# A gated cross-attention and expert block on one core: one start-up sum moved from VectorE to accumulating DMAs, three pieces of TensorE's order moved, and the last output add split

## The reference, cut to what matters

```python
x = x + tanh(g_xattn[0]) * attention(layernorm(x), ctx, wq, wk, wv, wo, q_norm_w, k_norm_w)
x = x + tanh(g_ffn[0])   * experts(layernorm(x), A, B, Wr)

# attention: x (16, 128, 1024), ctx (16, 128, 1024), 32 query heads, 8 key heads of 128
q, k = rmsnorm(x @ wq.T), rmsnorm(ctx @ wk.T)      # per head
out  = softmax(q @ k.T / sqrt(128)) @ (ctx @ wv.T)
return out @ wo.T
# experts: 64 experts of rank 16, the 16 best of a token are used
gates = softmax(top_k(x @ Wr.T, 16));  h = x @ A.T        # (tokens, 64 * 16)
return 2 * (h * gates) @ B
```

## Time and profile before

| | us |
|---|---|
| median of 3 runs (2317.69 to 2320.09) | 2319.02 |
| the profiled execution | 2318.4 |
| its span, first to last instruction | 2316.6 |
| PE busy | 2261.6 |
| DVE busy | 1597.6 |
| ACT busy | 1183.9 |
| POOL busy | 1144.8 |
| mean granted clock of PE, share of 2.4 GHz | 0.997 |

### The profile page before, as it was taken

The page is one execution under the profiler, slowest core; times in us unless marked ns, Lnnn a source line. Parts: engine busy times, 40 slices in busy tenths (PEclk is TensorE's granted clock), DMA queues, the critical chain, the costliest instruction groups (busy, mean ns, idle before and its releaser), DMA issues.

```text
span 2316.6 us, 35630 instructions
## 1 busy us (share of the span) xinstructions
PE 2261.6 (98%) x11615; PEld 1906.0 (82%) x11615; DVE 1597.6 (69%) x2669; ACT 1183.9 (51%) x3773; POOL 1144.8 (49%) x1735
## 2 busy tenths in 40 slices
PE   6999999999999999999999999999999999999999
PEld 5887887888888878888888788888888887888787
DVE  7558558777777797777777954755756878555755
ACT  5546546666666676666666732422424335333421
POOL 3666566666555555555555453233232664534221
PEclk9999999999999999999999999999999999999999
DMA  5688466767667367764322635645557566323643
GB/s 198 218 245 296 150 197 232 212 165 204 183 170 191 121 212 205 230 179 128 110 91 92 209 100 164 182 127 166 162 152 216 186 217 255 128 92 136 237 164 136
DMA packets 177062, 408.78 MB, mean 176 GB/s; under 512 B 11824, under 2 KB 77616, under 8 KB 159664
## 3 DMA queue, kind: packets, MB, share of 16 engines
q1 hardware_dynamic: 169392, 351.97, 44.1%
q0 software_dynamic: 7488, 54.53, 12.9%
HBM read 282.72 MB, written 190.84 MB: 204 GB/s over the span
## 4 chain that ended last, share of the span: by engine, by line
PE 84%; DVE 4%; POOL 4%; issue 3%; ACT 3%; DMA 2%; SPq 0%; POOLq 0%; ACTq 0%; DVEq 0%
PE bank L769 23%; PE bank L771 23%; PE bank L770 23%; PE bank L827 4%; PE bank L835 2%; PE bank L815 2%; DVE t_lo L1320 1%; PE bank L852 1%; PE bank L851 1%; PE bank L850 1%; ACT t_hi L1024 1%; POOL s_hi L1811 1%; DVE s_lo L1320 1%; DMA t_raw<-combos 1%; DMA staged<-in_w_q 1%
## 5 line engine op out<-in xcount | busy, mean ns | idle before, releaser
L769 PE MATMUL bank<-t_hi,s_hi 128*128 128x512 f32 x2688 | 1084.0, 403 | 30.7 <-DVE t_lo L1320 17.3
L771 PE MATMUL bank<-t_hi,s_lo 128*128 128x512 f32 x2688 | 1053.8, 392 | 0.0
L770 PE MATMUL bank<-t_lo,s_hi 128*128 128x512 f32 x2688 | 1050.9, 391 | 0.0
L769 PEld LDWEIGHTS bank<-t_hi,s_hi 128*128 128x128 f32 x2688 | 507.2, 189 | 128.1 <-issue 32.3
L771 PEld LDWEIGHTS bank<-t_hi,s_lo 128*128 128x128 f32 x2688 | 505.8, 188 | 110.7
L1320 DVE TENSOR_TENSOR s_lo<-staged,s_hi 128x512 fp32r<-128x512 f32 x672 | 525.0, 826 | 88.9 <-ACT s_hi L1035 86.9
L770 PEld LDWEIGHTS bank<-t_lo,s_hi 128*128 128x128 f32 x2688 | 507.5, 189 | 90.3
L1035 ACT CAST s_hi<-staged 128x512 fp32r<-128x512 f32 x434 | 250.2, 623 | 184.9 <-POOL staged L1801 71.5
L1782 POOL TENSOR_SCALAR small<-small 128x4 f32<-128x4 f32 (+1 forms) x192 | 75.9, 395 | 446.9 <-ACT small L1131 341.4
L1799 POOL TENSOR_TENSOR staged<-staged 128x512 f32<-128x512 f32 x86 | 115.3, 1340 | 365.5 <-DMA staged<-heads 196.9
L1463 DVE SCALAR_TENSOR_TENSOR probs<-bank,small,mask 128x128 f32<-128x128 f32 x512 | 143.9, 343 | 87.1 <-POOL small L1789 43.6
(11 more groups left out here) (143 smaller groups left out, 2894.7 us busy)
## 6 DMA issues: line engine op xcount, KB each, us to landing
heads<-heads SPq DMA_DIRECT2D x128, 256.0 KB, 4.3
staged<-in_w_q SPq DMA_DIRECT2D x32, 768.0 KB, 5.2
staged<-heads SPq DMA_DIRECT2D x32, 768.0 KB, 6.9
sums<-sums POOLq DMA_DIRECT2D x24, 1024.0 KB, 8.0
t_raw<-in_sets SPq DMA_DIRECT2D x20, 1024.0 KB, 7.1
t_raw<-combos SPq DMA_DIRECT2D x19, 1024.0 KB, 8.6
xt<-x_columns SPq DMA_DIRECT2D x8, 1792.0 KB, 6.8
combos<-in_sets POOLq DMA_DIRECT2D x14, 1024.0 KB, 10.2
```

The source lines that it names most:

```text
L769: nc.tensor.matmul(out, s_hi[w][:, cols], high, start=start, stop=False, skip_group_check=True)
L770: nc.tensor.matmul(out, s_hi[w][:, cols], low, start=False, stop=False, skip_group_check=True)
L771: done = nc.tensor.matmul(out, s_lo[w][:, cols], high, start=False, stop=at == 3, skip_group_check=True)
```

## The change

Five edits:

1. Tile 6 of the first set: `b21` is loaded straight into `t_raw[6]`, and POOL issues three accumulating transfers of 1 MB from DRAM into it (pieces 2, 3 and 0), each after the one before it has landed (`t4_added`). DVE's sum (line 1625) goes. ACT's `first_t(6)` waits for all three.
2. Transposes of the keys and of the first half of the x rows stand after product 3 instead of 2 in entries 8 and 9.
3. In entry 80 the router stands after product 4, the transpose of the scores after product 5, and DVE's `choose(0, 0)` in the slot of product 6.
4. The scratch tensor `xt` is laid out by partition, so that a tile of sets 2 and 3 is read in pieces of 8 KB instead of four of 2 KB.
5. In the last entry the `usum` part of the last result is scaled and added early, and the bank part straight from PSUM.

```diff
-        self.xt = scratch("xt", 2, 7, 4, P, HALF)
+        self.xt = scratch("xt", 2, 7, P, 4, HALF)
...
+    def router_beat(e):
+        return 4 if e == A0 else 3
...
-                src = d.xt[tau - 2, k].rearrange("a p c -> p a c")
+                src = d.xt[tau - 2, k]
...
             if tau == 1:
-                sp.wait_ge(t0_combo, 4)
                 src = weights(1, 0)
...
-        sp.dma_start(b21_again[:, :, :], b_in[1]).then_inc(again_in[1], 16)
+        sp.dma_start(t_raw[6][:, :, :], b_in[1]).then_inc(again_in[1], 16)
...
-                if e and j == 2:
+                if e and j == (3 if e in (8, 9) else 2):
                     key_columns(e - 1, 0)
                     x_columns(e - 1, 0)
...
-                if j == 3:
+                if j == router_beat(e):
                     router(e - A0)
-                if j == 4:
+                if j == router_beat(e) + 1:
                     score_rows(e - A0)
...
-                act.wait_ge(t0_combo, {2: 1, 3: 2, 1: 3, 6: 4}[k])
+                if k == 6:
+                    act.wait_ge(t4_added, 48)
+                else:
+                    act.wait_ge(t0_combo, {2: 1, 3: 2, 1: 3}[k])
...
+                if j == router_beat(e) + 1:
+                    router_scores(e - A0)
                 if j == 4:
-                    router_scores(e - A0)
                     rank_tile(e - A0)
...
+                if i == PAIRS - 1:
+                    nc.vector.scalar_tensor_tensor(yr[b][1][:, left], usum[:, :], tg2[:, :], yr[b][1][:, left], ALU.mult, ALU.add).then_inc(y_part, 1)
+            if j == 7 and i == PAIRS - 1:
+                dve.wait_ge(prod, plan.prod[e, 6])
+                dve.wait_ge(y_part, 1)
+                nc.vector.scalar_tensor_tensor(yr[b][1][:, left], bank[3][:, :], tg2[:, :], yr[b][1][:, left], ALU.mult, ALU.add).then_inc(y_set, 1)
...
-        dve.wait_ge(again_in[1], 16)
-        dve.wait_ge(t0_combo, 3)
-        nc.vector.tensor_tensor(t_raw[6][:, :, :], b21_again[:, :, :], t_raw[1][:, :, :], ALU.add).then_inc(t0_combo, 1)
         first_t(1)
...
+                if j == router_beat(e) + 2:
                     choose(i, 0)
...
+        def first_set_sum():
+            for n, b in enumerate((2, 3, 0)):
+                if n:
+                    pool.wait_ge(t4_added, 16 * n)
+                else:
+                    pool.wait_ge(again_in[1], 16)
+                nc.gpsimd.dma_start(t_raw[6][:, :, :], d.sets[0, b].rearrange("p (k c) -> p k c", k=4), accum_op=ALU.add,
+                                    max_dma_last_dim=8192).then_inc(t4_added, 16)
+
         sums(0)
+        first_set_sum()
```

More of the change, by code:

```diff
@@ L274, in program @@
     xo = m.put("x_columns", [P, 7, 4, S])
-    b11_again, b21_again = m.over("b11_again", [P, 4, HALF], xo_at), m.over("b21_again", [P, 4, HALF], pc_at)
+    b11_again = m.over("b11_again", [P, 4, HALF], xo_at)
     first_ahead = m.over("first_ahead", [P, 4, HALF], pc_at)
@@ L325, in program @@
     again_in, b12_in = [sem(f"again_in{w}") for w in range(2)], sem("b12_in")
+    y_part = sem("y_part")
     t_hi_done, t_lo_done, t0_combo = sem("t_hi_done"), sem("t_lo_done"), sem("t0_combo")
+    t4_added = sem("t4_added")
     st_in, st12_in = sem("staged_in"), sem("staged12_in")
@@ L481, in load_first_ahead @@
                 sp.wait_ge(xt_out, 64)
-                src = d.xt[0, 0].rearrange("a p c -> p a c")
+                src = d.xt[0, 0]
             sp.dma_start(first_ahead[:, :, :], src).then_inc(first_ahead_in, 16)
@@ L555, in columns_out @@
             sp.wait_ge(xo_pool, 2 * u + 2)
-            sp.dma_start(d.xt[u // 4, :, u % 4].rearrange("k p c -> p k c"), xo[:, :, :, :].rearrange("p k b q -> p k (b q)")).then_inc(xt_out, 16)
+            sp.dma_start(d.xt[u // 4, :, :, u % 4].rearrange("k p c -> p k c"), xo[:, :, :, :].rearrange("p k b q -> p k (b q)")).then_inc(xt_out, 16)
         def heads_out(w):
@@ L1597, in y_rows @@
                 nc.vector.scalar_tensor_tensor(yr[b][0][:, right], ct[1][:, :], tg2[:, :], yr[b][0][:, right], ALU.mult, ALU.add).then_inc(y_set, 1)
-            if j == 7:
+                if i == PAIRS - 1:
[4 more added lines that the diff above has]
+                nc.vector.scalar_tensor_tensor(yr[b][1][:, left], bank[3][:, :], tg2[:, :], yr[b][1][:, left], ALU.mult, ALU.add).then_inc(y_set, 1)
+            elif j == 7:
                 result21(e, ct[2][:, :])
@@ L1603, in first_t @@
         def first_t(k):
-            if k in (1, 3):
-                dve.wait_ge(t0_combo, 4 if k == 1 else 3)
+            if k == 3:
+                dve.wait_ge(t0_combo, 3)
             dve.wait_ge(t_hi_done, plan.t_fill(0, k))
```

## The result

| | before | after |
|---|---|---|
| median of 6 runs each, us | 2317.97 (2317.28 to 2320.09) | 2327.18 (2325.74 to 2327.85) |
| the profiled execution, us | 2318.4 | 2327.46 |
| its span, us | 2316.6 | 2325.7 |
| mean granted clock of PE | 0.997 | 0.995 |

The ratio is 1.0038, with an interval of 1.0028 to 1.0048: slower by 9.2 us. The forecast's sum was 2325.1, slower.

A forecast was written before the change was run, and what follows sets the result against it. PE bounds the kernel, busy 2261.6 of 2316.6 us. The terms 8.4 + 1.9 - 1.7 - 1.8 - 0.7 = +6.1 gave 2324.5 from the profiled execution, 2325.1 with the runs' median; range 2317.5 to 2331, the forecast's own 2321.5 to 2329.

The forecast's parts named there:

- Edit 1, what goes: At the start, removing DVE's addition of 2.28 us gains 0, since PE is held by its own spare matmuls.
- The first issue at 21.7: At the start, POOL issues the first accumulating transfer when piece b21 has landed, at 21.7 us.
- The first transfer, 9.0: At the start, the first accumulating transfer takes 9.0 us, since the last start-up loads are still arriving.
- The other two, 8.0 each: At the start, the second and third accumulating transfers take 8.0 us each, so tile 6 is whole at 46.7.
- Cast, `t_lo`, bank: 5.1: From landing at 46.7, adding 1.9, 2.3 and 0.9 puts product 6 at 51.8 against 43.39: +8.4 us.
- The clock, +1.9: PE idles 9.5 us before product 6 and drops to 1.2 GHz, costing 1.9 us; bounds 0 and 2.
- Edit 3, -1.8: In entry 80, `choose` moved behind the `s_lo` PE waits for gives -1.8 us; filling the router gap alone gives nothing.
- Edit 5, -0.7: At the end, the addition goes and the scaling starts at 2312.01, giving -0.7 us.
- A (nearly hidden): Rival at the start: transfers cost only 5.75 us each, product 6 at 44.1, kernel at 2315.5; chance 0.12.
- B (the moved pieces give nothing): Rival in entries 9 and 80: the wait only turns up a product later, kernel at 2328.6; chance 0.12.
- C (the issues are held up): Rival at the start: POOL's issues are stretched by 1 to 2 us each, +3 to +4, 2329; chance 0.11.
- D: Rival at the start: the third wait is met early, or a piece runs together; chance 0.02.

The follow-up runs named there:

- The two-transfer kernel: The changed kernel with two accumulating transfers instead of three, piece 0 left out of tile 6 of the first set; 2318.37 us, ratio 1.0004.

## Why the prediction was right

The sign, the mechanism and the place were right: PE's new wait is at product 6, it is released through DVE's `t_lo`, ACT's cast and the third transfer, and edit 1 alone carries it. The time, 2327.2, lies 2.1 above the forecast's sum and inside its own range. The sum against the profiled execution was +6.1 and came out as +9.1. It came that near partly by luck: the start was 3.4 too low, edit 3 gave 0.9 less than taken, and 1.1 us that lies in the profile of before alone hid part of it. Term by term:

- **Edit 1, what goes: 0.** Right. Product 5 starts at 39.45 against 39.39; DVE's 2.28 us turned into idle time (`usum` waits 3.77 instead of 1.41).
- **The first issue at 21.7.** Right, 21.89.
- **The first transfer, 9.0. This is the term that was off most.** It took 11.3 from issue to landing, 11.59 to the next issue: 2.6 more than taken, over the 10.2 that was to be its upper bound. Its packets began 4.0 us after the issue, 2.4 later than those of an undisturbed one, behind the loads of the start. The forecast allowed 1 us for this "since the last start-up loads are still arriving" and did not look at how long they would. The window of 22 to 26 us of the kernel before shows the DMA engines at 1.00 and the queue empty at about 26.8; 26.8 plus 8 would have given 34.8. It was 33.2, which is 1.6 less: so much passes between an issue and its first packet, and here it passed beside the loads. With one load held back it took 8.4.
- **The other two, 8.0 each.** Right: 8.29 and 8.24 from start to start. The rows of SBUF to DRAM were a good price for DRAM to SBUF.
- **Cast, `t_lo`, bank: 5.1 from landing to product 6.** Right: 50.01 to 55.16 is 5.15. So the start cost 11.8 instead of 8.4.
- **The clock, +1.9.** 1.54, as the mechanism had it; product 6 began at 0.43 a matmul, and with the wait filled by spares the 1.5 are gone. The two-transfer kernel shows that the price does not grow with the wait: 3.64 of idle time cost more afterwards, 2.7.
- **Edit 2.** Entry 8 gave 0 as said; entry 9 -1.95 against -1.7.
- **Edit 3, -1.8.** Mis-sized: -0.93. The forecast took `choose`, 1.8 us of DVE, as the gain of PE. But PE had waited only 0.76 us for that `s_lo`; once the wait is gone, PE's own work sets the start of entry 81, and the rest of the 1.8 is slack of DVE. Nor did the router's move help: the 2.94 ahead of the router came back as 1.75 ahead of product 4 and 1.08 ahead of the transposes of `x_rows`, in the rows at 1977.59 and 1987.25, 2.83 together. Before, the second of these did not show, because PE got there late from the router.
- **Edit 4.** Taken as 0; no run has it by itself, so it is only not contradicted.
- **Edit 5, -0.7.** The sum is gone, but relative to PE's last wait, at the start of entry 90 (2197.19, now 2206.72), DVE's last instruction starts 0.47 earlier and the span ends 0.43 earlier: the last matmuls themselves came 0.25 later. Where these 0.25 come from stays open.
- **The rivals.** A (nearly hidden) needed a transfer under 7.2 us; the adding ones took 8.0 and more, and only the plain ones would do. B (the moved pieces give nothing): wrong for entry 9, for entry 80 half true, since the wait ahead of the router only turned up later but the moved `choose` gave something. C (the issues are held up): they took 1.05, 0.88 and 0.86, no stretch. D: all three issues are there, each behind the landing of the one before.
- **Not in the forecast.** 1.1 us lie in the profile of before alone, between 847 and 931; they have no part in the change. Without it the profiles would differ by 10.2, and the medians differ by 9.2.

## What to carry to other kernels

Taking a sum off an engine gives nothing where that engine is waited for by nobody: here 2.28 us of DVE gave 0, and the transfers in its place cost 11.8. Price each transfer from landing rows of the same kind, and for the first of a series look at the DMA share in the window of its issue: here it began to move only as the loads issued before it ran out. Three adding transfers in series were a chain of 28 us from the first issue to the cast, which only a stage of that length hides. Before counting an engine's saved time as a gain, read how long the next engine really waited for it (0.76 us, not 1.8), and where a wait is filled, ask what the same engine waits for next: here it was a row of DVE that the first wait had covered. And before a wait in one profile is put down to an edit, look for it in the profiles without that edit: the wait at the second set was in some of them.

## What the runs showed of the hardware

- An accumulating transfer of 1 MB from DRAM into SBUF, alone on the engines, took 8.0 to 8.3 us; a plain one on the same queue 4.9 to 5.4. Per packet of 8 KB it was 629 against 309 ns, and with an adding one the DMA engines were busy for 0.70 of the time at 128 GB/s. Issuing it on POOL took 0.86 to 1.05 us, a plain one 0.53 to 0.75.
- A transfer issued by POOL at 21.9 moved nothing before 25.9 while SP's loads were queued: where an undisturbed one began 1.6 after its issue. It cost 3 us whether the transfer added or not.
- Holding one load back did not save its time, it moved it: the second transfer took 11.0 behind it, with its first packets 4.5 after the issue.
- PE's clock fell to the lower level in the window around a wait of 3.6 us (0.51 over 7 us), and in two profiles around waits of 2.9 in entry 80 (0.66 over 5 us), where the kernel before stayed at 1.00 behind the same wait of 2.94. Where it falls is not the same from profile to profile. What a stretch costs depends on how much of it lies in matmuls: 1.5 us where 3.3 did, 2.7 where 5.8 did.
- With PE kept busy by spare matmuls up to 0.17 us before product 6, the clock stayed at 1.00 and the 1.5 us were not lost.
